# A recommender tower on one core: low parts of three tables on GpSimd, a second lookup in pieces, six groups of rows turned between the products

## The chip, the cores and the metric

The kernel runs on one NeuronCore of a Trainium2 chip. The metric is the device time of one execution, in microseconds (us), lower is better. Three executions of the kernel before took 121.43, 120.68 and 122.37 us; the median is 121.43 us. The engines are TensorE (PE in the profile, its weight loads PEld), VectorE (DVE), ScalarE (ACT), GpSimd (POOL) and SyncE (SP, which issues transfers).

## The reference, cut to what matters

```python
# ids (512, 26); tbl_f (1000, 1250, 12500 or 125000 rows, 128), float32; dense (512, 128)
e = jnp.stack([tbl_f[ids[:, f]] for f in range(26)], axis=1)      # (512, 26, 128)
combined = jnp.concatenate([dense[:, None, :], e], axis=1)        # (512, 27, 128)
interactions = jnp.einsum('bnd,bmd->bnm', combined, combined)     # 27 x 27 per sample
z = jnp.concatenate([dense, interactions[:, TRIU_I, TRIU_J]], axis=1)
h = jnp.concatenate([z, dense], axis=1)                           # (512, 607)
h = jnp.maximum(h @ W_top1 + b_top1, 0.0)                         # 512 wide
h = jnp.maximum(h @ W_top2 + b_top2, 0.0)                         # 256 wide
y = h @ W_top3                                                    # (512, 1)
```

## The kernel before, in words

**Fifteen tables by products with one-hot matrices.** The 15 tables with 1000 or 1250 rows (`ONEHOT_TABLES`) are looked up on PE. Table number h is loaded whole, with 125 partitions of 8 or 10 rows each (`CHUNKS`). DVE compares the ids with row numbers (L544) and makes all chunks of the one-hot matrix but the last, which ACT makes (L620, L625). Tables that share one comparison form a unit (`UNITS`), and there are two buffers of one-hot matrices (`UNIT_RING`). To keep float32 precision each table is cut in two: ACT rounds it into a HIGH part (L610), and DVE subtracts that from the table, which gives the LOW part (`make_low`, L553, two halves per table). A lookup of a table of 8 chunks is 16 matmuls of 128 x 512: HIGH of the first half, LOW of the first half, HIGH of the second, LOW of the second (`lookup`, L355). There are two buffers of parts (`WORK_RING`) and four of tables (`TABLE_RING`): SP loads table h + 4 when both LOW halves of table h are made. ACT copies each finished lookup from PSUM into `xt` (L631). The last lookup (h = 14) is made in two pieces of 256 samples each (`COLUMNS`), so that the products of the first samples can start between parts of the second piece.

**Eleven tables by gathers.** GpSimd gathers rows of the other 11 tables with indirect transfers (L327), 4 tiles of 128 samples x 11 = 44 of them, in order. The rows are turned on PE by 3 or 4 transposes per group (`turn_group`, L370), 12 groups in all, 3 per tile; ACT copies each group into `xt` (L638). There are two PSUM banks for groups: group g may be turned once group g - 2 is copied. `AFTER_LOOKUP` lists which group is turned after which lookup, `BETWEEN_PRODUCTS` those turned later.

**Products and layers.** Each tile of 128 samples has 128 products 27 x 27 on PE in four quarters (`gram`, L392). DVE transposes the result of a tile in 32 x 32 blocks (L571) and packs the triangle (L576); the first quarter of the next tile waits for that transpose, since the PSUM banks are the same. PE turns z (`turn_z`, L403), ACT copies it (L647), and the three layers follow (L416 and L426, L440 or L453, L466), tile by tile, woven into the products of the tiles behind.

**Order.** Every engine works through a list written in the program, in order, and waits on semaphores. On GpSimd the list is the four row-number instructions and then the 44 gathers back to back; gather number n (from n = 6, every third) may not start before a certain lookup is done (`GATHERS_AHEAD`, `GATHERS_PER_LOOKUP`).

Of the kernel before, what the change touches and what calls it, by code (L numbers as in the profile page):

```python
# [57 lines left out]
UNITS = [[0], [1, 2], [3], [4, 5], [6], [7, 8], [9], [10, 11], [12], [13, 14]]  # L58
# [25 lines left out]
COLUMNS = [[(0, B)]] * (NOH - 1) + [[(0, B // 2), (B // 2, B)]]  # L84
PIECES = NOH + 1
# [11 lines left out]
AFTER_LOOKUP = [[], [], [], [0], [1], [2], [3], [4], [5], [], [6], [7], [8], [9], []]  # L97
BETWEEN_PRODUCTS = [10, 11]
# [51 lines left out]
def build(nc, dense_by_column, ids, ids_by_table, tables, w1, w2, columns, identity, out):  # L150
    with ExitStack() as ctx:
# [123 lines left out]
        def _(sp):  # L275
            def load_table(h):
# [7 lines left out]
                if h >= TABLE_RING:  # L284
                    sp.wait_ge(part_ready[LOW], 2 * (h - TABLE_RING + 1))
# [47 lines left out]
        def _(pe):  # L333
            def lookup(h, piece=0, quarters=range(4)):
# [5 lines left out]
                if h + piece >= 2 and 0 in quarters:  # L340
                    pe.wait_ge(lookup_copied, h + piece - 1)
                for half in range(2):
                    for part in PARTS:
# [4 lines left out]
                        else:  # L348
                            pe.wait_ge(part_ready[LOW], 2 * h + 1 + half)
                        for c in range(half * chunks // 2, (half + 1) * chunks // 2):  # L350
# [176 lines left out]
        def _(dve):  # L527
# [73 lines left out]
        def _(act):  # L601
# [137 lines left out]
```

## Time and profile before

| what | value |
|---|---|
| three runs, median | 121.43 us (120.68 to 122.37) |
| profiled execution, its own time | 120.86 us |
| its span, first to last instruction | 118.8 us |
| mean granted TensorE clock | 0.971 of full |
| PE busy | 110.5 us, 93% |
| DVE busy | 72.8 us, 61% |
| ACT busy | 59.2 us, 50% |
| POOL busy | 52.5 us, 44% |

The profile is of one execution; times in it are counted from the start of its span. The shares are means over stages with different limits: lookups until 71 us, products of the first two tiles until 87 us, then the rest of the products and the layers.

### The profile page before, as it was taken

How to read it: one execution, taken by the hardware profiler on the slowest of the kernel's cores; microseconds unless marked ns; L12 is line 12 of the kernel's file. 1: busy time of each engine (PE TensorE's matmuls, PEld its weight loads, DVE VectorE, ACT ScalarE, POOL GpSimd, SP SyncE). 2: the span in 40 equal slices, each digit the busy share in tenths (PEclk: the TensorE clock that was granted, in tenths of full speed). 3: DMA queues.
4: the chain of work that ended last, by engine and by line, in shares of the span. 5: the costliest groups of instructions: out<-in, count | busy, mean ns of one | idle time of the engine just before them, and what ended most of it. 6: DMA issues, size and time to landing. Idle time of an engine off the chain costs nothing.

```text
span 118.8 us, 3660 instructions
## 1 busy us (share of the span) xinstructions
PE 110.5 (93%) x1573; PEld 90.3 (76%) x1573; DVE 72.8 (61%) x160; ACT 59.2 (50%) x111; POOL 52.5 (44%) x52
## 2 busy tenths in 40 slices
PE   5999999979999999999997999766999999999991
PEld 2377578848888888888885899654799999999970
DVE  3799999999899997999399700070072053044020
ACT  3729967994497776790999050301020211113441
POOL 2777778778877777778777700000000000000000
PEclk9999999999999999999999999985599999999999
DMA  4899999999996799649942200000000000000000
GB/s 87 283 303 282 279 256 258 246 273 247 268 263 138 199 258 257 159 92 337 397 145 50 61 22 6 6 0 6 6 6 6 6 0 6 6 6 0 0 0 1
DMA packets 6044, 15.48 MB, mean 130 GB/s; under 512 B 1655, under 2 KB 2427, under 8 KB 5902
## 3 DMA queue, kind: packets, MB, share of 16 engines
q1 hardware_dynamic: 4452, 12.20, 36.9%
q0 software_dynamic: 1408, 2.89, 9.9%
q10 hardware_dynamic: 170, 0.18, 0.7%
q8 instruction: 12, 0.20, 0.6%
q14 instruction: 2, 0.02, 0.1%
HBM read 15.26 MB, written 0.00 MB: 129 GB/s over the span
## 4 chain that ended last, share of the span: by engine, by line
PE 83%; DVE 9%; issue 3%; DMA 2%; ACT 1%; DVEq 0%
PE ps_a L355 46%; PE ps_gram L392 10%; DVE onehot L544 6%; PE ps_rows L426 5%; PE ps_h L440 5%; PE ps_a L426 5%; PE ps_rows L370 5%; DMA idrow<-ids_by_table 2%; PE ps_rows L416 2%; PE ps_z L403 2%; PE ps_a L453 2%; DVE part_sb L553 2%; PE ps_a L416 1%; DVE table_sb L571 1%; PE ps_h L466 1%
## 5 line engine op out<-in xcount | busy, mean ns | idle before, releaser
L355 PE MATMUL ps_a<-onehot,part_sb 125*128 125x512 f32 (+1 forms) x272 | 63.6, 386 | 1.9 <-issue 1.7
L327 POOL DMA_INDIRECT rows_sb<-tbl,ids_sb x44 | 51.9, 1179 | 15.3 <-issue 13.1
L355 PEld LDWEIGHTS ps_a<-onehot,part_sb 125*128 125x128 f32 x272 | 47.7, 188 | 13.7 <-issue 4.0
L544 DVE TENSOR_SCALAR onehot<-idrow,row_id 125x512 fp32r<-125x512 int16 (+1 forms) x78 | 42.2, 602 | 2.6 <-DMA idrow<-ids_by_table 1.5
L553 DVE TENSOR_TENSOR part_sb<-table_sb,part_sb 125x512 fp32r<-125x512 f32 (+1 forms) x30 | 20.6, 716 | 2.0 <-ACT part_sb L610 2.0
L571 DVE STREAM_TRANSPOSE table_sb<-ps_gram 128x864 f32<-128x864 f32 x4 | 4.3, 1083 | 26.6 <-PE ps_gram L392 26.6
L631 ACT COPY xt<-ps_a 128x512 f32<-128x512 f32 (+1 forms) x16 | 10.0, 628 | 19.0 <-PE ps_a L355 11.9
L610 ACT CAST part_sb<-table_sb 125x1024 fp32r<-125x1024 f32 (+2 forms) x16 | 16.8, 1056 | 2.7 <-DMA table_sb<-tbl 2.7
L392 PE MATMUL ps_gram<-xt 128*27 128x27 f32 x1024 | 13.1, 201 | 2.8 <-issue 2.1
L392 PEld LDWEIGHTS ps_gram<-xt 128*27 128x27 f32 x1024 | 11.1, 114 | 5.6 <-issue 4.2
L638 ACT COPY xt<-ps_rows 128x128 f32<-128x128 f32 (+2 forms) x32 | 8.2, 340 | 5.6 <-PE ps_rows L370 5.4
L620 ACT ACTIVATE distance<-idrow,row_id 125x512 f32<-125x512 int16 (+1 forms) x10 | 9.5, 948 | 0.2 <-DMA idrow<-ids_by_table 0.2
L625 ACT ACTIVATE onehot<-distance 125x512 fp32r<-125x512 f32 (+1 forms) x10 | 8.5, 848 | 0.8
L647 ACT COPY table_sb<-ps_z 128x384 f32<-128x384 f32 x4 | 1.9, 479 | 12.0 <-PE ps_z L403 12.0
L370 PE MATMUL ps_rows<-ident_sb,rows_sb 128*128 128x128 f32 x44 | 7.2, 284 | 0.0
L370 PEld LDWEIGHTS ps_rows<-ident_sb,rows_sb 128*128 128x128 f32 x44 | 5.7, 145 | 1.4
L440 PE MATMUL ps_h<-table_sb,w_sb 128*128 128x128 f32 x48 | 6.5, 279 | 0.0
L426 PE MATMUL ps_a<-table_sb,w_sb 128*128 128x128 f32 x48 | 6.1, 279 | 0.0
L426 PE MATMUL ps_rows<-table_sb,w_sb 128*128 128x128 f32 x48 | 6.1, 279 | 0.0
L440 PEld LDWEIGHTS ps_h<-table_sb,w_sb 128*128 128x128 f32 x48 | 5.8, 192 | 0.1
L474 PE MATMUL ps_z<-zeros 128*128 128x512 bf16 x13 | 4.6, 526 | 1.2 <-DVE zeros L528 1.2
L426 PEld LDWEIGHTS ps_a<-table_sb,w_sb 128*128 128x128 f32 x48 | 5.6, 192 | 0.1
(33 smaller groups left out, 44.4 us busy)
## 6 DMA issues: line engine op xcount, KB each, us to landing
table_sb<-tbl SPq DMA_DIRECT2D x11, 448.0 KB
table_sb<-tbl SPq DMA_DIRECT2D x4, 560.0 KB
idrow<-ids_by_table SPq DMA_DIRECT2D x5, 256.0 KB
w_sb<-w SPq DMA_DIRECT2D x1, 1280.0 KB
rows_sb<-tbl,ids_sb POOLq DMA_INDIRECT x44
table_sb<-tbl SPq DMA_DIRECT2D x10, 52.0 KB
idrow<-ids_by_table SPq DMA_DIRECT2D x4, 128.0 KB
w_sb<-w SPq DMA_DIRECT2D x1, 512.0 KB
```

What stands on the lines that cost most here:

```text
L327: pool.indirect_dma_start(rows_sb[:, t % ROWS_RING, GATHERED.index(f), :], None, tables[f], bass.IndirectOffsetOnAxis(ids_sb[:, t, f:f + 1 ...
L355: last = pe.matmul(ps_a[:, (h + piece) % 2, a:b], parts_sb[part][:, w, c * D:(c + 1) * D], unit_onehot(u, c)[:, member, a:b], start=(part ...
L370: last = pe.transpose(ps_rows[:, g % 2, slot * P:(slot + 1) * P], rows_sb[:, t % ROWS_RING, GATHERED.index(n - 1), :], ident)
L392: last = pe.matmul(ps_gram[j * NPAD:j * NPAD + N, half, s * N:(s + 1) * N], x, x, start=True, stop=True)
L426: last = pe.matmul(h1_block(t, m), w1_sb[:, c, m * P:(m + 1) * P], zt[:, t % 2, c, :], start=False, stop=(c == ZC - 1), skip_group_check=True)
L440: last = pe.matmul(h2_block(t, m), w2_sb[:, k, m * P:(m + 1) * P], h1[:, t % 2, k, :], start=(k == 0 and m == 0), stop=(k == M1 - 1), skip ...
L544: dve.tensor_scalar(unit_onehot(u, c), idrow[0:VP, w, 0:n, :], row_id[0:VP, first + c:first + c + 1], None, ALU.is_equal).then_inc(onehot_ ...
L553: dve.tensor_tensor(parts_sb[LOW][:, w, columns], table_sb[0:VP, s, columns], parts_sb[HIGH][:, w, columns].bitcast(F32), ALU.subtract).th ...
L610: act.copy(parts_sb[HIGH][:, w, first:end], table_sb[0:VP, s, first:end]).then_inc(part_ready[HIGH], 1)
L620: act.activation(distance[:, 0:n, :], idrow[0:VP, w, 0:n, :], ACT.Abs, bias=row_id[0:VP, negated:negated + 1]) \
L625: act.activation(unit_onehot(u, chunks - 1), distance[:, 0:n, :], ACT.Relu, bias=1.0, scale=-1.0) \
L631: act.copy(xt[:, a // RUN:b // RUN, ONEHOT_TABLES[h] + 1, :], ps_a[:, (h + piece) % 2, a:b].rearrange("p (q r) -> p q r", r=RUN)).then_inc ...
```

## The change

GpSimd makes the LOW parts of tables h = 0, 5 and 12 (`LOW_BY_GPSIMD`), two subtractions of 125 x 512 each, put into its list ahead of its 3rd, its 20th and its 41st gather. DVE no longer makes them. The tables are reordered (table 7, of 1250 rows, moves from place 12 to place 10), so the chunks per lookup and the units change with them, and h = 12 now has 8 chunks. Lookups 13 and 14 are both made in two pieces. Six groups of rows (6 to 11) are turned behind the lookups instead of two. `GATHERS_AHEAD` goes from 6 to 9. The total number of chunks stays 128.

The list of GpSimd in the kernel before, from its branch to its end (`rows_sb` holds gathered rows, `row_id` the row numbers):

```order
L308 UNCONDITIONAL_BRANCH
L313 ISA
L313 IOTA row_id 128x8
L315 IOTA row_id 128x1
L313 IOTA row_id 128x10
L315 IOTA row_id 128x1
L327 DMA rows_sb<-tbl,ids_sb 128x128 x44
L151 UNCONDITIONAL_BRANCH
```

The same list after the change, from the last row-number instruction on (`part_sb` holds the parts, `table_sb` the tables):

```order
L336 IOTA row_id 128x1
L361 DMA rows_sb<-tbl,ids_sb 128x128 x2
L344 TENSOR_TENSOR part_sb<-table_sb,part_sb 125x512 x2
L361 DMA rows_sb<-tbl,ids_sb 128x128 x17
L344 TENSOR_TENSOR part_sb<-table_sb,part_sb 125x512 x2
L361 DMA rows_sb<-tbl,ids_sb 128x128 x21
L344 TENSOR_TENSOR part_sb<-table_sb,part_sb 125x512 x2
L361 DMA rows_sb<-tbl,ids_sb 128x128 x4
L167 UNCONDITIONAL_BRANCH
```

Six subtractions stand in the one list of GpSimd now: the pair of table 5 behind 19 gathers, the pair of table 12 behind 40.

The list of PE in the kernel before, from lookup 13 to the last quarter of tile 1 (L355 lookups, L370 transposes of groups, L392 products, L416 the dense part of layer 1, L403 the turning of z):

```order
L355 MATMUL ps_a<-onehot,part_sb 128x512 x16
L370 MATMUL ps_rows<-ident_sb,rows_sb 128x128 x4
L355 MATMUL ps_a<-onehot,part_sb 128x256 x24
L392 MATMUL ps_gram<-xt 27x27 x32
L355 MATMUL ps_a<-onehot,part_sb 128x256 x4
L392 MATMUL ps_gram<-xt 27x27 x32
L355 MATMUL ps_a<-onehot,part_sb 128x256 x4
L370 MATMUL ps_rows<-ident_sb,rows_sb 128x128 x4
L392 MATMUL ps_gram<-xt 27x27 x32
L416 MATMUL ps_a<-dense_sb,w1d 128x128 x2
L392 MATMUL ps_gram<-xt 27x27 x32
L416 MATMUL ps_a<-dense_sb,w1d 128x128 x2
```

The same place after the change, from the lookups 9 to 12 (72 matmuls, no group between them) to the second quarter of tile 1 (L389 lookups, L404 transposes, L426 products, L450 the dense part):

```order
L389 MATMUL ps_a<-onehot,part_sb 128x512 x72
L389 MATMUL ps_a<-onehot,part_sb 128x256 x44
L426 MATMUL ps_gram<-xt 27x27 x32
L389 MATMUL ps_a<-onehot,part_sb 128x256 x4
L404 MATMUL ps_rows<-ident_sb,rows_sb 128x128 x4
L426 MATMUL ps_gram<-xt 27x27 x32
L389 MATMUL ps_a<-onehot,part_sb 128x256 x8
L426 MATMUL ps_gram<-xt 27x27 x32
L404 MATMUL ps_rows<-ident_sb,rows_sb 128x128 x4
L389 MATMUL ps_a<-onehot,part_sb 128x256 x4
L426 MATMUL ps_gram<-xt 27x27 x32
L389 MATMUL ps_a<-onehot,part_sb 128x256 x4
```

The last four matmuls of the last piece now stand behind the whole of tile 0, and group 8 and then the first quarter of tile 1 follow them. On ACT the copies of groups 6 to 11 stand behind the copy of that last piece. The diff, cut to its core:

```diff
-ONEHOT_TABLES = [4, 10, 11, 0, 17, 19, 1, 20, 24, 5, 25, 3, 7, 8, 14]
+ONEHOT_TABLES = [4, 10, 11, 0, 17, 19, 1, 20, 24, 5, 7, 25, 3, 8, 14]
-CHUNKS = [8] * 3 + ([10] + [8] * 2) * 4
+CHUNKS = [8] * 3 + ([10] + [8] * 2) * 2 + [10] * 2 + [8] * 4
-UNITS = [[0], [1, 2], [3], [4, 5], [6], [7, 8], [9], [10, 11], [12], [13, 14]]
+UNITS = [[0], [1, 2], [3], [4, 5], [6], [7, 8], [9], [10], [11, 12], [13, 14]]
+LOW_BY_GPSIMD = {0: 2, 5: 19, 12: 40}
...
-COLUMNS = [[(0, B)]] * (NOH - 1) + [[(0, B // 2), (B // 2, B)]]
+SPLIT = 2
+COLUMNS = [[(0, B)]] * (NOH - SPLIT) + [[(0, B // 2), (B // 2, B)]] * SPLIT
...
-AFTER_LOOKUP = [[], [], [], [0], [1], [2], [3], [4], [5], [], [6], [7], [8], [9], []]
-BETWEEN_PRODUCTS = [10, 11]
+AFTER_LOOKUP = [[], [], [0], [1], [2], [], [3], [4], [5], [], [], [], [], [], []]
+BETWEEN_PRODUCTS = [6, 7, 8, 9, 10, 11]
-GATHERS_AHEAD = 6
+GATHERS_AHEAD = 9
...
@@ SP, load_table
-                    sp.wait_ge(part_ready[LOW], 2 * (h - TABLE_RING + 1))
+                    sp.wait_ge(low_ready(h - TABLE_RING), low_number(h - TABLE_RING, 1))
@@ GpSimd
+            def make_low(h):
+                s, w, middle = h % TABLE_RING, h % WORK_RING, CHUNKS[h] // 2 * D
+                if h >= WORK_RING:
+                    pool.wait_ge(lookup_done, h - WORK_RING + 1)
+                for half, columns in enumerate((slice(0, middle), slice(middle, CHUNKS[h] * D))):
+                    pool.wait_ge(part_ready[HIGH], rounded(h, half))
+                    pool.tensor_tensor(parts_sb[LOW][:, w, columns], table_sb[0:VP, s, columns],
+                                       parts_sb[HIGH][:, w, columns].bitcast(F32), ALU.subtract) \
+                        .then_inc(low_by_gpsimd_ready, 1)
...
+                    for h, gather in LOW_BY_GPSIMD.items():
+                        if gather == issued:
+                            make_low(h)
@@ PE, lookup
-                            pe.wait_ge(part_ready[LOW], 2 * h + 1 + half)
+                            pe.wait_ge(low_ready(h), low_number(h, half))
@@ PE, behind the lookups
-            lookup(NOH - 1, 1, [0, 1])
+            lookup(before, 1, [0, 1, 2])
             gram(0, 0)
-            lookup(NOH - 1, 1, [2])
+            lookup(before, 1, [3])
+            turn_group(BETWEEN_PRODUCTS[0])
             gram(0, 1)
-            lookup(NOH - 1, 1, [3])
-            turn_group(BETWEEN_PRODUCTS[0])
+            lookup(last, 1, [0, 1])
             gram(0, 2)
-            layer1_dense(0, 0)
+            turn_group(BETWEEN_PRODUCTS[1])
+            lookup(last, 1, [2])
             gram(0, 3)
-            layer1_dense(0, 1)
+            lookup(last, 1, [3])
+            turn_group(BETWEEN_PRODUCTS[2])
             gram(1, 0)
-            turn_group(BETWEEN_PRODUCTS[1])
+            for k in range(2):
+                layer1_dense(0, k)
             gram(1, 1)
-            layer1_dense(1, 0)
+            turn_group(BETWEEN_PRODUCTS[3])
             gram(1, 2)
             turn_z(0)
+            for g in BETWEEN_PRODUCTS[4:]:
+                turn_group(g)
             gram(1, 3)
-            layer1_dense(1, 1)
+            for k in range(2):
+                layer1_dense(1, k)
@@ DVE
-            dve.wait_ge(part_ready[LOW], 2 * NOH)
+            dve.wait_ge(part_ready[LOW], 2 * (NOH - len(LOW_BY_GPSIMD)))
+            dve.wait_ge(low_by_gpsimd_ready, 2 * len(LOW_BY_GPSIMD))
```

## Rows read from the trace of the kernel before

**Rows 1.** The chain that ended last, 13 to 76 us: start, length, what.

```profile
13.02 10.04 PE ps_a L355 x42
...
24.40 0.81 issue
25.21 3.07 PE ps_a L355 x12
28.28 0.44 PE ps_rows L370 x4
28.72 3.64 PE ps_a L355 x16
32.36 0.33 PE ps_rows L370 x3
32.69 4.57 PE ps_a L355 x20
...
64.38 0.70 issue
...
68.54 2.87 PE ps_a L355 x24
71.41 0.68 PE ps_gram L392 x54
72.09 0.67 PE ps_a L355 x4
```

**Rows 2.** The same chain, 76 us to the layers.

```profile
76.56 1.04 issue
...
77.85 1.09 DVE table_sb L571
...
81.53 1.09 issue
82.62 0.34 PE ps_gram L392 x9
82.95 1.16 PE ps_rows L416 x4
84.11 0.90 PE ps_gram L392 x64
85.01 0.83 PE ps_z L403 x3
...
87.30 1.34 PE ps_a L426 x12
...
94.67 0.89 PE ps_a L416 x8
...
100.67 0.48 PE ps_z L403 x3
```

**Rows 3.** Stretches: us, PE, PEld, DVE, ACT, POOL busy (instructions), granted clock, DMA share, GB/s.

```profile
74.00:77.00 3.00, 2.56 (x137) 2.13 (x134) 0.00 (x0) 1.13 (x4) 0.00 (x0) 1.00 0.02 5
77.00:79.00 2.00, 0.85 (x5) 0.63 (x5) 1.11 (x2) 0.00 (x0) 0.00 (x0) 1.00 0.00 0
79.00:81.00 2.00, 1.92 (x95) 1.56 (x99) 1.00 (x9) 0.23 (x1) 0.00 (x0) 0.64 0.03 8
81.00:83.00 2.00, 0.91 (x57) 0.73 (x45) 0.00 (x0) 0.31 (x1) 0.00 (x0) 0.50 0.00 0
83.00:85.00 2.00, 2.00 (x69) 1.72 (x69) 0.00 (x0) 0.00 (x0) 0.00 (x0) 0.50 0.03 8
85.00:87.00 2.00, 2.00 (x72) 1.63 (x71) 0.26 (x1) 0.48 (x1) 0.00 (x0) 0.65 0.00 0
```

**Rows 4.** Waits: engine and line, whom it waited for, us, times, longest.

```profile
POOL rows_sb L327 <- issue: 13.1, 43, 0.3
```

**Rows 5.** Timeline of POOL: gathers 1, 11, 19, 20, 40 and 41 of 44.

```profile
3.46 1.12 POOL L327 DMA_INDIRECT rows_sb<-tbl,ids_sb  x1 [2.22 <-DMA ids_sb<-ids]
...
18.48 2.26 POOL L327 DMA_INDIRECT rows_sb<-tbl,ids_sb  x1 [0.30 <-issue]
...
31.32 1.56 POOL L327 DMA_INDIRECT rows_sb<-tbl,ids_sb  x1 [0.30 <-issue]
33.19 1.02 POOL L327 DMA_INDIRECT rows_sb<-tbl,ids_sb  x1 [0.30 <-issue]
...
62.23 1.02 POOL L327 DMA_INDIRECT rows_sb<-tbl,ids_sb  x1 [0.30 <-issue]
63.55 1.02 POOL L327 DMA_INDIRECT rows_sb<-tbl,ids_sb  x1 [0.30 <-issue]
```

**Rows 6.** Groups by form: line, engine, operation, count; busy us, mean ns; idle before.

```profile
L327 POOL DMA_INDIRECT rows_sb<-tbl,ids_sb x44 | 51.9, 1179 | 15.3 <-issue 13.1 <-DMA ids_sb<-ids 2.2
...
L553 DVE TENSOR_TENSOR part_sb<-table_sb,part_sb 125x512 fp32r<-125x512 f32 x22 | 14.4, 680 | 0.0
```

**Rows 7.** Timeline of DVE: comparisons for two tables of 8, a pair of subtractions.

```profile
19.84 4.72 DVE L544 TENSOR_SCALAR onehot<-idrow,row_id 125x1024 fp32r<-125x1024 int16 x7
24.48 1.28 DVE L553 TENSOR_TENSOR part_sb<-table_sb,part_sb 125x512 fp32r<-125x512 f32 x2
```

**Rows 8.** Timeline of ACT: copies of a piece and of a group of four.

```profile
68.87 0.79 ACT L638 COPY xt<-ps_rows 128x128 f32<-128x128 f32 x4
70.50 0.40 ACT L631 COPY xt<-ps_a 128x256 f32<-128x256 f32 x1 [0.83 <-PE ps_a L355]
```

**Rows 9.** Stretch 8.8 to 13.7 us, columns as in rows 3.

```profile
8.80:13.70 4.90, 4.73 (x19) 2.86 (x18) 4.90 (x9) 4.84 (x6) 3.99 (x4) 1.00 1.04 264
```

More of the change, by code:

```diff
@@ L74 @@
         _places[_c] = _places.get(_c, []) + [(_members[0], half)]
+    _places = {_c: [(h, half) for h, half in halves if h not in LOW_BY_GPSIMD] for _c, halves in _places.items()}
     LOW_BEFORE.append(_places)
     _owed = _members[1:]
-LOW_AT_END = [(h, half) for h in _owed for half in range(2)]
+LOW_AT_END = [(h, half) for h in _owed for half in range(2) if h not in LOW_BY_GPSIMD]
 VP_A = VP // 16 * 16
@@ L82, with place @@
 ROWS_RING = 2
-COLUMNS = [[(0, B)]] * (NOH - 1) + [[(0, B // 2), (B // 2, B)]]
-PIECES = NOH + 1
+SPLIT = 2
+COLUMNS = [[(0, B)]] * (NOH - SPLIT) + [[(0, B // 2), (B // 2, B)]] * SPLIT
+PIECES = NOH + SPLIT
+def place(h, piece):
+    return h + SPLIT * piece
 GATHERED = [f for f in range(F) if f not in ONEHOT_TABLES]
@@ L103, with low_number @@
 GATHERS_PER_LOOKUP = 3
-GATHERS_AHEAD = 6
+GATHERS_AHEAD = 9
 HIGH, LOW = PARTS = range(2)
+def low_number(h, half):
+    same = [x for x in range(h) if (x in LOW_BY_GPSIMD) == (h in LOW_BY_GPSIMD)]
+    return 2 * len(same) + 1 + half
 def rounded(h, half):
@@ L217, in build @@
         part_ready = [sem(f"part{i}_ready") for i in PARTS]
+        low_by_gpsimd_ready = sem("low_by_gpsimd_ready")
         lookup_done = sem("lookup_done")
@@ L234, in build, with low_ready @@
         stored = sem("stored")
+        def low_ready(h):
+            return low_by_gpsimd_ready if h in LOW_BY_GPSIMD else part_ready[LOW]
         def unit_onehot(u, c):
@@ L339, in lookup @@
                 a, b = COLUMNS[h][piece]
-                if h + piece >= 2 and 0 in quarters:
-                    pe.wait_ge(lookup_copied, h + piece - 1)
+                if place(h, piece) >= 2 and 0 in quarters:
+                    pe.wait_ge(lookup_copied, place(h, piece) - 1)
                 for half in range(2):
@@ L354, in lookup @@
                                 pe.wait_ge(last_onehot_ready, u + 1)
-                            last = pe.matmul(ps_a[:, (h + piece) % 2, a:b], parts_sb[part][:, w, c * D:(c + 1) * D],
+                            last = pe.matmul(ps_a[:, place(h, piece) % 2, a:b], parts_sb[part][:, w, c * D:(c + 1) * D],
                                              unit_onehot(u, c)[:, member, a:b], start=(part == HIGH and c == 0),
@@ L381, in gram @@
                     pe.wait_ge(group_copied, GROUPS_UP_TO[t])
-                    pe.wait_ge(lookup_copied, NOH + (t >= TILES // 2))
+                    pe.wait_ge(lookup_copied, NOH if t < TILES // 2 else PIECES)
                     if t == 0:
@@ L480, in _ @@
                     turn_group(g)
-            lookup(NOH - 1, 1, [0, 1])
+            before, last = NOH - 2, NOH - 1
+            lookup(before, 1, [0, 1, 2])
             gram(0, 0)
-            lookup(NOH - 1, 1, [2])
+            lookup(before, 1, [3])
+            turn_group(BETWEEN_PRODUCTS[0])
             gram(0, 1)
-            lookup(NOH - 1, 1, [3])
-            turn_group(BETWEEN_PRODUCTS[0])
+            lookup(last, 1, [0, 1])
             gram(0, 2)
-            layer1_dense(0, 0)
+            turn_group(BETWEEN_PRODUCTS[1])
+            lookup(last, 1, [2])
             gram(0, 3)
-            layer1_dense(0, 1)
+            lookup(last, 1, [3])
+            turn_group(BETWEEN_PRODUCTS[2])
             gram(1, 0)
-            turn_group(BETWEEN_PRODUCTS[1])
+            for k in range(2):
+                layer1_dense(0, k)
             gram(1, 1)
-            layer1_dense(1, 0)
+            turn_group(BETWEEN_PRODUCTS[3])
             gram(1, 2)
             turn_z(0)
+            for g in BETWEEN_PRODUCTS[4:]:
+                turn_group(g)
             gram(1, 3)
-            layer1_dense(1, 1)
+            for k in range(2):
+                layer1_dense(1, k)
             for t in range(TILES - 2):
@@ L628, in copy_lookup @@
             def copy_lookup(h, piece=0):
-                act.wait_ge(lookup_done, h + piece + 1)
+                act.wait_ge(lookup_done, place(h, piece) + 1)
                 a, b = COLUMNS[h][piece]
                 act.copy(xt[:, a // RUN:b // RUN, ONEHOT_TABLES[h] + 1, :],
-                         ps_a[:, (h + piece) % 2, a:b].rearrange("p (q r) -> p q r", r=RUN)).then_inc(lookup_copied, 1)
+                         ps_a[:, place(h, piece) % 2, a:b].rearrange("p (q r) -> p q r", r=RUN)).then_inc(lookup_copied, 1)
             def copy_group(g):
@@ L693, in _ @@
                     copy_group(g)
-            copy_lookup(NOH - 1, 1)
+            for h in range(NOH - SPLIT, NOH):
+                copy_lookup(h, 1)
             for g in BETWEEN_PRODUCTS:
```

## The prediction

> **What bounds the kernel now.** I read the chain that ended last first [rows 1]. From 13.02 us on it is PE: lookups at 3.64 us per 16 matmuls, which is 0.2275 us each, transposes of groups at 0.44 for four. Two gaps "issue" stand in it, 0.81 at 24.40 and 0.70 at 64.38; in both PE stands between the HIGH and the LOW matmuls of a lookup, so I read them as waits for a LOW part. So until 71 us PE is the limit and DVE comes close to it.
>
> Behind that stage PE loses more [rows 2]: 1.04 at 76.56, a wait for DVE's transpose (1.09 at 77.85), 1.09 at 81.53. The granted clock falls too [rows 3]: 0.64, 0.50, 0.50 and 0.65 in the four stretches from 79 to 87 us. PE had been busy 0.85 of 2.00 us ahead of it. At that level (1.2 GHz) a quarter of products took 0.90 us instead of 0.68, three transposes of z 0.83 instead of 0.48, the dense four 1.16 where eight took 0.89 later. Over the whole low stretch I put the loss at 2.5 us. With 2.8 us of gaps (1.04, 1.09 and 0.6 of the wait for DVE) the change has 5.3 us to win there.
>
> Last I read GpSimd's own line, because the change puts work into its list. It waits for nothing: 43 idle times of 0.30 us each [rows 4], so its 44 gathers run back to back from 3.46 us, mean 1179 ns [rows 5, 6]. The 20th starts at 33.19 and the 41st at 63.55: a 44% share of the span, yet a full list until 68 us.
>
> **GpSimd's chain, the term that decides.** The subtractions of table 5 stand where gather 20 stood, those of table 12 where gather 41 stood. No row has a subtraction on GpSimd. The bounds: DVE's same operation on the same shape takes 680 ns [rows 6]; the longest thing GpSimd does, a gather, 2.26 us [rows 5]. I take 1.2 us each with its gap, the mean of what that engine did here: a software-driven engine is nearer to its own row than to DVE's. The Trainium skill (GPSIMD Engine Reference, § Performance versus the Vector engine) gives 4497 ns for 2048 float32 elements of a tensor_tensor; a quarter is an estimate of 1.12 us, and by it the forecast falls by five times 0.08.
>
> - LOW of table 5, first half: 33.19 + 2 x 1.2 (table 0's pair, ahead of it) + 1.2 = 36.8 us.
> - LOW of table 12, first half: 63.55 + 4 x 1.2 + 1.2 = 69.55 us.
>
> When does PE want them? Lookup 5 ran from 28.72; its LOW matmuls come after four HIGH ones, at 29.63. Group 2 (0.33) is now ahead of it, and up to 0.8 is saved before, at the gap of 24.40 or the start. So PE wants table 5 at 28.8 to 30.0 and stands still about **7 us**. All that DVE's relief gives before this point (the subtractions of tables 0 and 5, 1.28 us a pair [rows 7]) is lost in that wait.
>
> From 36.8 at the full clock: the other 12 matmuls 2.73; lookups 6, 9 and 10 of 20 matmuls at 4.57; 7, 8 and 11 at 3.64; three groups 0.44 + 0.44 + 0.33; four HIGH of lookup 12, 0.91. Sum 29.5, so PE is at table 12's LOW at 66.3, and 69.55 is 3.3 us later. The clock will surely have fallen in a wait of 7 us, when 2.3 us of gaps were enough before. The low stretch before is 6.8 us long by rows 3; lookups at half the clock would lose at most 3.4 us in it. That loss fits into the 3.3 us of the second wait, so I cost it at nothing: GpSimd hides it. Queued behind: DVE's one-hot matrices run ahead by two units in the waits and then keep pace (a unit of two tables of 8 costs it 4.72 + 2 x 1.28 = 7.3 us [rows 7], as much as PE). SP's load of table 9 waits for table 5's LOW and comes some 6 us late, but its rounding is wanted at 50 us. The w1 load behind table 14 comes later too and is wanted only near 77.
>
> **After 69.55.** The other 12 matmuls of lookup 12: 2.73, so 72.3. Then 44 matmuls of 256 columns; 24 of them took 2.87, so 0.12 each, 5.27: the first products start at 77.55 instead of 71.41, **6.1 us later**. Splitting lookup 13 costs only 16 x (0.24 - 0.2275) = 0.2, and 0.2 per switch to products, inside these terms.
>
> From there to layer 1 (87.30 before, so 15.9 us): eight quarters of products at 0.68 = 5.4; pieces of 4, 8, 4 and 4 matmuls 3.2; 22 transposes at 0.11 = 2.4; the dense part 2 x 0.89 = 1.8; turning z 0.5. That is 13.3. One wait is new: group 8 may be turned only when group 6 is copied, and ACT copies it behind the last piece: 0.40 + 0.79 us [rows 8], 1.2 in all. DVE's transpose of tile 0 (1.09) runs under it. The gaps "issue" at 76.56 and 81.53 I let go, since products now lie between other work. With the clock up this stage takes 14.5 us, 1.4 less than before. Behind it both kernels do the same.
>
> Sum against the profiled execution's own 120.86 us: + 6.1 - 1.4 = 125.6. The median of the runs is 0.6 above that execution, so for the runs I say **126.0 us**, 3.8% slower. (Two per cent, 119.0 to 123.9, is about what a measurement of this kernel can tell from no change.)
>
> **Rivals.**
>
> 1. *GpSimd's subtractions are blocked by DVE.* At 2.26 us each, five of them lie 5.3 us later: 131. Against: between 8.8 and 13.7 us DVE was busy 4.90 of 4.90 us [rows 9] and four gathers took 3.99 us there. For: those gathers don't read two tables out of SBUF. During the pair of table 5 DVE should be idle itself. The Trainium skill (SBUF — State Buffer, § Who interferes with whom) says that a VectorE instruction in a 2-port mode, or with two SBUF inputs against a GpSimd instruction that reads SBUF, blocks the other for its whole length; by that rule each subtraction among comparisons could begin one DVE instruction late. Chance 0.15.
>
> 2. *The clock falls a second time.* If it is up again soon after 37 us, PE reaches table 12 at 67, waits 2 to 3 us and starts the pieces and products at the low level; by a loss of 2.5 (as before) to 3.4 us this gives 128.5 to 129.5. Chance 0.12.
>
> 3. *The gathers get shorter, and it is not slower.* A gather of 1.02 us with its gap is 1.32; the first 19 took 29.7 us, which is 4.6 more than 19 x 1.32, the first 40 took 60.1, which is 7.3 more. What makes some of them long I can't tell; the DMA share is at 1.04 in the first stage [rows 9], so it may be the transfers. If PE's wait thins these out, the chain shortens with them. Without any long gather, table 5 comes at 32.1, table 12 at 62.3, and the sum is 7.3 less: 118.7 for the runs, which is 2% faster. It decides from the point where that excess falls by half: then 122.3, within 2%. Against: the load of SP in the first 30 us is the same as before. Chance 0.08 for all of it, 0.10 for about half.
>
> 4. *The relief works as written:* GpSimd has the LOW parts before PE asks. Then only the gains are left, some 118. It would need 19 gathers and three subtractions by 29 us; at 1.32 and DVE's own 0.68 they end at 30.6. Not given a chance of its own.
>
> **How the numbers follow.** The forecast of 126 has 0.55. Its own range: GpSimd at 0.68 us would put table 12 at 66.9, but the slowed PE is there only at 68 to 69, so it can't fall below some 124.4; with long gathers a few tenths longer it reaches 127.5. The range for 8 in 10 takes in half of rival 3 below and most of rival 1 above: 122.0 to 131.0. Slower by over 2%: forecast and rivals 1 and 2, less a little, 0.79. Within 2%: 0.13. Faster: 0.08.
>
> **What would show it.** In the timeline of POOL, a pair of TENSOR_TENSOR behind gather 2, gather 19 (near 35.5 to 38 us) and gather 40 (near 68.3 to 70.8); their mean tells rival 1. In the chain of waits, a step to POOL's line L344 twice, and PE's line L389 waiting for it, near 7 us and up to 3.3 us. In the stretches, a granted clock of 0.5 after 33 us, full again by 44 us, and full from 79 to 93 us. PE should wait about 1.2 us at group 8 for ACT. If PE doesn't wait for table 5, or the gathers 3 to 19 end before 32 us, the forecast is wrong; if it waits as said and the time still isn't up by 3%, then the stage between the lookups and the layers gave back more than I count.

## The result, and the profile after

The changed kernel took 129.4 us (median of four runs, 128.6 to 129.93) against 121.36 us (120.68 to 122.37) for the kernel before: a ratio of 1.065, 95% interval 1.056 to 1.074. It is 6.5% slower; the forecast was 126.0 us with a range of 122.0 to 131.0. Medians here and below are of all runs of a kernel; ratios leave out runs more than 1.5% above its fastest. The profiled execution took 129.36 us, with a span of 127.6 us (118.8 before) and a mean granted clock of 0.973 (0.971 before).

First the page: busy time of each engine, and the granted clock in 40 slices of 3.19 us.

```profile
PE 113.9 (89%) x1589; PEld 92.0 (72%) x1589; DVE 73.0 (57%) x154; ACT 59.2 (46%) x112; POOL 60.0 (47%) x58
...
PEclk9999999999756999999999999999999999999999
```

DVE has six instructions less and is busy no shorter (72.8 before). The clock falls in slices 11 to 13, not near 80 us as before. The groups of section 5 and the views by form show the new operation, and what DVE did with its relief:

```profile
L344 POOL TENSOR_TENSOR part_sb<-table_sb,part_sb 125x512 fp32r<-125x512 f32 x6 | 7.6, 1285 | 0.3 <-ACT part_sb L652 0.2
...
L585 DVE TENSOR_SCALAR onehot<-idrow,row_id 125x1024 fp32r<-125x1024 int16 x35 | 27.5, 852 | 9.6 <-PE ps_a L389 8.3 <-DMA idrow<-ids_by_table 1.4
...
L594 DVE TENSOR_TENSOR part_sb<-table_sb,part_sb 125x512 fp32r<-125x512 f32 x16 | 10.5, 679 | 0.4 <-ACT part_sb L652 0.4
```

A subtraction takes 1285 ns on GpSimd. Six fewer on DVE are 3.9 us less than the 14.4 of [rows 6]. But the comparisons take 27.5 us for 35; the same 35 take 24.1 in a kernel that does without GpSimd's subtractions (first experiment). 3.4 of the 3.9 us are given back.

GpSimd's list, beside [rows 5]: the two pairs that PE waits for.

```profile
33.90 2.50 POOL L344 TENSOR_TENSOR part_sb<-table_sb,part_sb 125x512 fp32r<-125x512 f32 x2
...
67.65 2.52 POOL L344 TENSOR_TENSOR part_sb<-table_sb,part_sb 125x512 fp32r<-125x512 f32 x2
```

They run behind gathers 19 and 40, as written. The chain that ended last, to the start of the layers, beside [rows 1, 2]:

```profile
33.90 1.28 POOL part_sb L344
35.19 0.04 issue
35.23 10.04 PE ps_a L389 x32
...
64.75 7.31 DVE onehot L585 x7
72.06 0.60 DVE part_sb L594
72.67 0.04 issue
72.71 5.05 PE ps_a L389 x40
77.76 0.68 PE ps_gram L426 x52
...
84.57 0.45 issue
...
85.44 0.38 ACT xt L673
85.82 0.68 ACT xt L680 x4
86.50 0.04 issue
86.55 0.55 PE ps_rows L404 x3
...
87.77 1.09 PE ps_a L450 x8
...
89.42 0.73 issue
...
93.37 0.27 issue
...
95.15 1.34 PE ps_a L460 x12
```

Products start at 77.76 instead of 71.41, layer 1 at 95.15 instead of 87.30, and the span ends at 127.6 instead of 118.8. So the 8.8 us are 6.35 before the products, 1.5 in their first stage and 0.95 behind it. The chain's last leg ahead of the products is DVE's: its comparisons at 64.75 ran beside GpSimd's second pair, and its LOW part for lookup 13 came 0.24 us after PE could have used it. PE's own timeline at the two places, with the wait in brackets:

```profile
35.23 5.06 PE L389 MATMUL ps_a<-onehot,part_sb 125*128 125x512 f32 x11 [4.61 <-POOL part_sb L344]
...
68.99 3.48 PE L389 MATMUL ps_a<-onehot,part_sb 125*128 125x512 f32 x16 [0.84 <-POOL part_sb L344]
72.71 5.05 PE L389 MATMUL ps_a<-onehot,part_sb 125*128 125x256 f32 x40 [0.24 <-DVE part_sb L594]
```

Columns of the stretches are those of [rows 3]:

```profile
33.00:36.00 3.00, 0.77 (x2) 0.67 (x3) 0.00 (x0) 0.00 (x0) 2.98 (x3) 0.62 0.17 44
36.00:39.00 3.00, 3.00 (x9) 2.32 (x8) 0.00 (x0) 0.00 (x0) 2.31 (x3) 0.50 0.50 151
```

PE works through 36 to 39 us at the low level (0.50, 1.2 GHz); it had stood idle for 4.61 us before. The 32 matmuls that take 7.3 us at 0.2275 each took 10.04.

### The profile page after: what moved, and what is told of

Read it like the earlier page. It is cut to its first block, busy times and chain, and to the rows that moved or that the text cites. A ratio compares the mean times of both kernels' runs of the same rounds, so it can differ in the third digit from the quotient of the medians.

```text
span 127.6 us, 3698 instructions
## 1 busy us (share of the span) xinstructions
PE 113.9 (89%) x1589; PEld 92.0 (72%) x1589; DVE 73.0 (57%) x154; ACT 59.2 (46%) x112; POOL 60.0 (47%) x58
## 4 chain that ended last, share of the span: by engine, by line
PE 61%; DVE 19%; POOL 6%; DMA 5%; issue 5%; ACT 1%; DVEq 0%
PE ps_a L389 28%; DVE onehot L585 16%; PE ps_gram L426 9%; DMA idrow<-ids_by_table 5%; POOL rows_sb L361 5%; PE ps_rows L460 5%; PE ps_h L474 5%; PE ps_a L460 5%; PE ps_rows L404 3%; DVE part_sb L594 3%; PE ps_a L487 2%; PE ps_a L450 2%; PE ps_rows L450 2%; PE ps_z L437 1%; POOL part_sb L344 1%
## 5 line engine op out<-in xcount | busy, mean ns | idle before, releaser
L389 PE MATMUL ps_a<-onehot,part_sb 125*128 125x512 f32 (+1 forms) x288 | 67.1, 385 | 7.3 <-POOL part_sb L344 5.4
L389 PEld LDWEIGHTS ps_a<-onehot,part_sb 125*128 125x128 f32 x288 | 50.8, 195 | 20.6 <-POOL part_sb L344 6.7
L585 DVE TENSOR_SCALAR onehot<-idrow,row_id 125x512 fp32r<-125x512 int16 (+1 forms) x78 | 45.6, 648 | 11.3 <-PE ps_a L389 8.7
L594 DVE TENSOR_TENSOR part_sb<-table_sb,part_sb 125x512 fp32r<-125x512 f32 (+1 forms) x24 | 16.7, 724 | 1.1 <-ACT part_sb L652 1.1
L426 PE MATMUL ps_gram<-xt 128*27 128x27 f32 x1024 | 12.9, 194 | 1.5 <-issue 1.5
L426 PEld LDWEIGHTS ps_gram<-xt 128*27 128x27 f32 x1024 | 10.7, 107 | 4.2 <-issue 2.5
L404 PE MATMUL ps_rows<-ident_sb,rows_sb 128*128 128x128 f32 x44 | 6.8, 277 | 1.2 <-ACT xt L680 1.1
L344 POOL TENSOR_TENSOR part_sb<-table_sb,part_sb 125x512 fp32r<-125x512 f32 x6 | 7.6, 1285 | 0.3 <-ACT part_sb L652 0.2
L404 PEld LDWEIGHTS ps_rows<-ident_sb,rows_sb 128*128 128x128 f32 x44 | 5.1, 141 | 2.5 <-ACT xt L680 1.3
L508 PE MATMUL ps_z<-zeros 128*128 128x512 bf16 x13 | 5.5, 617 | 1.2 <-DVE zeros L569 1.2
```

The costliest lines, as they stand in the source:

```text
L344: pool.tensor_tensor(parts_sb[LOW][:, w, columns], table_sb[0:VP, s, columns], parts_sb[HIGH][:, w, columns].bitcast(F32), ALU.subtract) \
L389: last = pe.matmul(ps_a[:, place(h, piece) % 2, a:b], parts_sb[part][:, w, c * D:(c + 1) * D], unit_onehot(u, c)[:, member, a:b], start=(p ...
L404: last = pe.transpose(ps_rows[:, g % 2, slot * P:(slot + 1) * P], rows_sb[:, t % ROWS_RING, GATHERED.index(n - 1), :], ident)
L426: last = pe.matmul(ps_gram[j * NPAD:j * NPAD + N, half, s * N:(s + 1) * N], x, x, start=True, stop=True)
L585: dve.tensor_scalar(unit_onehot(u, c), idrow[0:VP, w, 0:n, :], row_id[0:VP, first + c:first + c + 1], None, ALU.is_equal).then_inc(onehot_ ...
L594: dve.tensor_tensor(parts_sb[LOW][:, w, columns], table_sb[0:VP, s, columns], parts_sb[HIGH][:, w, columns].bitcast(F32), ALU.subtract).th ...
```

## The experiments

All ratios are against the kernel before, run on the same chip beside each kernel, with 95% intervals. Its medians there lay between 121.72 and 122.52 us.

### Is it the part of GpSimd, or the new order?

**Everything of the change but GpSimd's subtractions.** DVE makes all LOW parts.

```diff
-LOW_BY_GPSIMD = {0: 2, 5: 19, 12: 40}
+LOW_BY_GPSIMD = {}
-            dve.wait_ge(low_by_gpsimd_ready, 2 * len(LOW_BY_GPSIMD))
```

> The change with all LOW parts made by VectorE again (no subtraction on GpSimd); the order of tables, the second lookup in pieces and the six groups between the products stay. Theory (GpSimd's list is what made the change slow): TensorE's wait of 4.6 us at table 5 and of 0.8 at table 12 are gone, the clock doesn't fall at 33 us, the comparisons that took 7.4 us beside GpSimd's subtractions take 4.7 again, and the first products start near 71 us instead of 77.7: 122 to 124 us. Rival (the new order behind the lookups is itself the loss): 126 us or more.

Measured: 120.43 us, ratio 0.984 (0.976 to 0.992), below the 122 to 124 that I had expected: the new order alone gains 1.6%. Products start at 68.28, 3.1 us before [rows 1]. Some 1.7 of that are the 15 transposes of groups that no longer stand between lookups, and the two waits for DVE are 0.31 and 0.24 instead of 0.81 and 0.70. Behind the lookups it loses again; PE's timeline there, at group 8:

```profile
77.37 0.60 PE L404 MATMUL ps_rows<-ident_sb,rows_sb 128*128 128x128 f32 x3 [1.15 <-ACT xt L679]
...
78.80 2.08 PE L450 MATMUL ps_a<-dense_sb,w1d 128*128 128x128 f32 x8
```

The wait for ACT comes 0.4 us behind a gap of 0.71 (75.13 to 75.84), and then the clock is at 0.50 from 78 to 81 us: the dense eight take 2.08 instead of 1.09. So without GpSimd's part the order pays, even with this loss in it.

**The reverse: the kernel before, with GpSimd's subtractions alone**, at the same three places and with `GATHERS_AHEAD` at 9 (`make_low` and its waits are those of the change; table 12 has 10 chunks here).

```diff
+LOW_BY_GPSIMD = {0: 2, 5: 19, 12: 40}
-GATHERS_AHEAD = 6
+GATHERS_AHEAD = 9
```

> The kernel before with the change's first part alone: LOW parts of tables 0, 5 and 12 by GpSimd at the same places in its list (and 9 gathers ahead); tables, pieces and groups as before. Table 12 has 10 chunks here, so its subtractions are of 125 x 640. Theory (that part alone is the whole loss): TensorE waits 4 to 5 us at table 5, reaches table 12 near GpSimd's 69 us, first products near 80 us, 128.5 to 131.5 us. Rival (the new order shares in the loss): under 127 us.

Measured: 132.26 us, ratio 1.091 (1.080 to 1.103), a little above the range that I had given. PE waits 4.75 us at table 5 and only 0.31 at table 12, but DVE comes late behind it:

```profile
66.72 7.80 DVE L578 TENSOR_SCALAR onehot<-idrow,row_id 125x1024 fp32r<-125x1024 int16 x7 [1.94 <-PE ps_a L389]
```

These seven took 4.72 in [rows 7]. They run beside GpSimd's pair (66.86, 3.11 us long), and PE then waits 1.70 us for DVE's LOW part at 75.16. So GpSimd's part alone costs 9.1%, more than the whole change: the order gives some back. (Part of that is table 12's pair, which is of 125 x 640 here.)

### Are the waits a matter of the place in GpSimd's list?

**Table 5's pair five gathers earlier**, then **table 12's pair four gathers earlier**, then **both**:

```diff
-LOW_BY_GPSIMD = {0: 2, 5: 19, 12: 40}
+LOW_BY_GPSIMD = {0: 2, 5: 14, 12: 40}
```

> The pair of table 5 stands behind 14 gathers instead of 19, that of table 12 still behind 40. Theory (one chain on GpSimd, and table 12's place in it is the wall): the wait at table 5 is gone (TensorE wants it near 30 us, GpSimd has it near 28.5), but TensorE then waits for table 12 until 69 us all the same, some 6 to 7 us long, and the clock falls in that wait, so that pieces and products run at 1.2 GHz: 129 to 132 us, no gain. Rival (each wait adds its own length): 129.4 less 4.6 and the 2.8 us lost by the clock, 122 us.

Measured: 131.67 us, ratio 1.077 (1.068 to 1.085). No wait at table 5, and the whole of it at table 12:

```profile
70.04 5.22 PE L389 MATMUL ps_a<-onehot,part_sb 125*128 125x512 f32 x14 [8.48 <-POOL part_sb L344]
```

Removing the larger wait of the two brought no gain. PE reached the second place earlier, stood there longer, and paid for the clock behind it (0.50 until 72 us, 0.62 from 72 to 75).

```diff
-LOW_BY_GPSIMD = {0: 2, 5: 19, 12: 40}
+LOW_BY_GPSIMD = {0: 2, 5: 19, 12: 36}
```

> The pair of table 12 stands behind 36 gathers instead of 40, that of table 5 still behind 19. Theory: the wait at table 5 stays (4.6 us), and so does the fall of the clock behind it; TensorE comes to table 12 near 68 us and finds it made: 0.8 us less, and up to 1 us more where the comparisons of the last unit are no longer held up at the same place: 127.5 to 129 us. Rival (table 12's subtraction holds VectorE, which is the real wall): 126 us or less.

Measured: 127.86 us (126.43 to 129.12, too scattered for an interval) beside 122.17. Table 5 still stops PE for 3.60 us, table 12 no longer, and products start at 75.47, 2.2 us before those of the change; the next wait, behind it, is for DVE:

```profile
70.48 5.06 PE L389 MATMUL ps_a<-onehot,part_sb 125*128 125x256 f32 x40 [0.81 <-DVE part_sb L594]
```

```diff
-LOW_BY_GPSIMD = {0: 2, 5: 19, 12: 40}
+LOW_BY_GPSIMD = {0: 2, 5: 14, 12: 36}
```

> Table 5 behind 14 gathers and table 12 behind 36. Theory: neither wait is left, the clock stays up in the lookups, the first products start near 71 to 72 us: 122 to 124.5 us. Rival (GpSimd's subtractions hold VectorE for their whole length, 1.28 us each, six of them): the lookups stay late by some 3 to 5 us, 125.5 to 128 us.

Measured: 127.03 us, ratio 1.038 (1.031 to 1.046). I had expected neither wait. But PE now comes to table 12 some 6 us earlier, and for that place 36 is still too late:

```profile
65.74 9.98 PE L389 MATMUL ps_a<-onehot,part_sb 125*128 125x512 f32 x56 [3.49 <-POOL part_sb L344]
```

My expectation had judged the new place by the old time of the reader.

**Place 32 for table 12**, so that nobody waits for GpSimd:

```diff
-LOW_BY_GPSIMD = {0: 2, 5: 19, 12: 40}
+LOW_BY_GPSIMD = {0: 2, 5: 14, 12: 32}
```

> Table 5 behind 14 gathers, table 12 behind 32. GpSimd should then have table 12 before TensorE wants it near 62 us. Theory (both waits were the loss, and VectorE pays for each subtraction of GpSimd with its length while it has little of that to spare): no wait for GpSimd above 0.5 us, first products at 69 to 71.5 us, 121 to 124 us, no better than with all LOW parts on VectorE (120.4). Rival (the relief of VectorE is worth something once it comes in time): 119 us or less.

Measured: 121.97 us (ten runs), ratio 1.005 (1.001 to 1.009). The waits for GpSimd are gone, and with them almost all of the loss. Still it is slower than the same order with no subtraction on GpSimd (0.984). The profile of DVE shows why:

```profile
26.45 6.32 DVE L585 TENSOR_SCALAR onehot<-idrow,row_id 125x512 fp32r<-125x512 int16 x9
...
57.65 6.87 DVE L585 TENSOR_SCALAR onehot<-idrow,row_id 125x1024 fp32r<-125x1024 int16 x7
```

Nine such comparisons take 3.70 where GpSimd only gathers, seven of the wide form 4.72. They ran beside GpSimd's two pairs and took 2.6 and 2.15 us longer; each pair had relieved DVE of 1.28. Over the whole kernel DVE's comparisons take 48.6 us, where they take 42.2 with no subtraction on GpSimd, and its subtractions of 125 x 512 take 10.4 instead of 14.5: 6.4 us more for 4.1 less. So well-timed pairs cost DVE more than they save it, and PE waits 0.84 us for DVE ahead of 65.17.

**Keep PE busy in the first wait.** The changed kernel, with 16 products of zeros ahead of PE's wait for table 5:

```diff
+                        elif h == 5 and half == 0:
+                            for _ in range(16):
+                                pe.matmul(ps_z[:, 0, :], zeros[:, 0:P], zeros[:, :], start=True, stop=True)
+                            pe.wait_ge(low_ready(h), low_number(h, half))
```

> The change as it is, with 16 more matmuls of 512 columns on zeros put ahead of TensorE's wait for table 5's LOW part (3.5 us of the 4.6 us wait), their result unused. Theory (table 12's place in GpSimd's list is the wall, so what the clock costs ahead of it is hidden): the clock stays up at 33 to 41 us, the 32 matmuls behind the wait take 7.3 instead of 10.0 us, TensorE waits some 3.5 us at table 12 instead of 0.8, first products still near 77.5 us, and the clock may fall there instead: 128.5 to 131.5 us. Rival (the slow clock behind the first wait is part of the loss): 126 to 127.5 us.

Measured: 132.29 us, ratio 1.083 (1.074 to 1.091), above the 128.5 to 131.5 expected and far from the rival's 126 to 127.5.

```profile
35.24 7.59 PE L393 MATMUL ps_a<-onehot,part_sb 125*128 125x512 f32 x32 [1.10 <-POOL part_sb L344]
...
69.14 11.03 PE L393 MATMUL ps_a<-onehot,part_sb 125*128 125x512 f32 x56 [3.50 <-POOL part_sb L344]
```

The clock stayed up (1.00 from 33 to 36 us) and the 32 matmuls took 7.59 instead of 10.04. But PE resumed at table 12 at 69.14, as without them (68.99): the 2.5 us were spent waiting there. So the step of the prediction that costs the first clock loss at nothing is shown to be right. The new wait of 3.50 us then brought the clock down (0.50 from 69 to 72 us) just before the products, which start at 80.10: that is the second fall of rival 2, and its price comes on top. In the change itself this fall did not happen (1.00 from 69 to 72 and from 77 to 96 us).

### Who blocks whom?

**Six subtractions on GpSimd that nobody waits for**, added to the order with DVE making all (the first experiment), at places 2, 19 and 40, on memory of their own.

```diff
+                    for _ in range(2 if issued in (2, 19, 40) else 0):
+                        pool.wait_ge(idle_done, idle)
+                        pool.tensor_tensor(idle_out[0:VP, :], idle_in[0:VP, :], idle_in[0:VP, :],
+                                           ALU.subtract).then_inc(idle_done, 1)
+                        idle += 1
```

> VectorE makes all LOW parts, and GpSimd makes six subtractions of 125 x 512 on a buffer of its own that nobody waits for, at the change's places (ahead of gathers 3, 20 and 41). So only the place in the list and the sharing with VectorE are left of the suspected cost. Theory (a subtraction on GpSimd holds VectorE for its length): single comparisons or subtractions of VectorE beside them grow by 1.3 to 2.6 us, GpSimd's own stay at 1.28, gathers end some 8 us later; in time 0.5 to 3 us more than without them (120.4). Rival (VectorE is not held): its operations keep their lengths, and the time stays at 120 to 121.

Measured: 124.77 us, ratio 1.029 (1.021 to 1.037), where the same kernel without them has 0.984. Work on GpSimd that nobody uses costs 4.5 points, more than I had expected; the products start at 72.83 instead of 68.28. It is not that gathers come later: PE waits for none of them, but 4.0 us in all for DVE's LOW parts. DVE's timeline and then GpSimd's:

```profile
3.47 5.09 DVE L592 TENSOR_SCALAR onehot<-idrow,row_id 125x512 fp32r<-125x512 int16 x7 [1.38 <-DMA idrow<-ids_by_table]
...
34.45 5.94 DVE L592 TENSOR_SCALAR onehot<-idrow,row_id 125x1024 fp32r<-125x1024 int16 x7 [0.28 <-PE ps_a L396]
...
67.22 3.44 DVE L601 TENSOR_TENSOR part_sb<-table_sb,part_sb 125x512 fp32r<-125x512 f32 x2 [0.49 <-ACT part_sb L658]
```

```profile
6.04 2.24 POOL L364 TENSOR_TENSOR idle_out<-idle_in 125x512 f32<-125x512 f32 x2
33.15 3.37 POOL L364 TENSOR_TENSOR idle_out<-idle_in 125x512 f32<-125x512 f32 x2
67.61 2.50 POOL L364 TENSOR_TENSOR idle_out<-idle_in 125x512 f32<-125x512 f32 x2
```

Without them the three rows of DVE read 2.90, 4.73 and 1.28: +2.2, +1.2 and +2.2 us. At 67.61 DVE's second subtraction waits while GpSimd's pair keeps its 2.50; at 33.15 both pay, GpSimd 0.9 and DVE 1.2. The Trainium skill (SBUF — State Buffer, § Who interferes with whom) has the port pair as an exclusive lock held for a whole instruction by whoever issued first, and a tensor_tensor with both inputs in SBUF as one that contends with GpSimd's reads. The third pair agrees: 3.44 against 1.28. For the comparisons, with one input in SBUF, the page allows it only in a 2-port mode; no row names the mode they run in. The rows do show that they work at twice the rate of the subtractions: a comparison takes 0.26 us more for 512 more columns (0.67 against 0.41), a subtraction 0.13 us more for 128 (0.81 against 0.68).

### The stage behind the lookups

**Groups 7 and 8 each turned one place later** in the order with DVE making all, so that ACT's copies are done when PE wants the bank:

```diff
             gram(0, 2)
-            turn_group(BETWEEN_PRODUCTS[1])
             lookup(last, 1, [2])
             gram(0, 3)
             lookup(last, 1, [3])
-            turn_group(BETWEEN_PRODUCTS[2])
+            turn_group(BETWEEN_PRODUCTS[1])
             gram(1, 0)
+            turn_group(BETWEEN_PRODUCTS[2])
             for k in range(2):
                 layer1_dense(0, k)
```

> As the version in which VectorE makes all LOW parts, with groups 7 and 8 turned one place later: 7 behind the last piece, 8 behind the first quarter of tile 1. Theory (TensorE's 1.15 us at group 8 is ScalarE's copying of group 6 behind the last piece): that wait is gone, 0.2 to 0.5 us of waiting for VectorE's transpose of tile 0 comes in its place, and with less idling the clock may stay up between 79 and 86 us, worth up to 2.5 us: 117.5 to 120 us. Rival (TensorE only waits elsewhere for ScalarE, since all copies stand behind that piece): 120 to 121 us, as before the edit.

Measured: 118.15 us (117.75 to 119.87), ratio 0.973 (0.963 to 0.983): the fastest kernel of the study. PE no longer waits for ACT's copies and the clock is 1.00 for the whole span of 115.7 us. What is left are gaps with no releaser inside runs of products:

```profile
78.79 0.31 PE L426 MATMUL ps_gram<-xt 128*27 128x27 f32 x14 [0.80 <-issue]
...
82.55 0.42 PE L426 MATMUL ps_gram<-xt 128*27 128x27 f32 x29 [0.53 <-issue]
```

The first comes behind 50 of 64 matmuls of that quarter, the second behind 35, and the changed kernel has its gaps of 0.73 and 0.27 at the same two counts.

**Shift PE's list by 64 instructions** in that kernel (three warm-up matmuls fewer, 35 tiny ones more, each with its weight load), to see whether the gaps belong to data or to the place in the code:

```diff
-            for _ in range(WARM_UP):
+            for _ in range(WARM_UP - 3):
...
+            for _ in range(35):
+                pe.matmul(ps_z[:, 0, 0:NPAD], zeros[:, 0:P], zeros[:, 0:NPAD], start=True, stop=True)
```

> The fastest version so far (VectorE makes all LOW parts, group 8 behind the first quarter of tile 1; 118.15 us) with 3 of the 13 warm-up matmuls taken away and 35 of 32 columns put in their place, so that 64 more TensorE instructions (32 matmuls and their weight loads) lie ahead of everything. In that version, in the one with group 8 earlier and in the change, gaps that nothing releases stand at the same points of TensorE's list: 50 matmuls into the second quarter of tile 1, 35 into its fourth. Theory (they come with the loading of TensorE's code in blocks of 16 KB): the gaps move 32 matmuls earlier in the list, to about 18 and 3 matmuls into those quarters; time 117.5 to 119.5 us. Rival (they belong to the place: a PSUM bank or a copy): they stay at 50 and 35.

Measured: 119.89 us, ratio 0.979 (0.974 to 0.984).

```profile
80.09 0.59 PE L426 MATMUL ps_gram<-xt 128*27 128x27 f32 x46 [1.09 <-issue]
...
83.85 0.72 PE L426 MATMUL ps_gram<-xt 128*27 128x27 f32 x61 [0.50 <-issue]
```

The gaps moved by 32 matmuls, behind 18 and behind 3. The time is a little above what I had expected, and above that of the kernel without the shift, because more gaps come to light: they add up to 3.8 us here (1.10 at 71.51 in tile 0, 0.36 at 87.88 and 0.71 at 100.12 besides these two), 1.9 us there. The run with PE kept busy in the first wait has 16 more matmuls ahead of everything, and shifts the two gaps by 16, from behind 50 and 35 to behind 34 and 19:

```profile
92.05 0.42 PE L430 MATMUL ps_gram<-xt 128*27 128x27 f32 x30 [1.12 <-issue]
...
96.08 0.59 PE L430 MATMUL ps_gram<-xt 128*27 128x27 f32 x45 [0.81 <-issue]
```

So the gaps belong to the place in PE's list, not to an operand. Neighbouring gaps stand 126 to 128 matmuls apart, which is 252 to 256 instructions with their weight loads. A page of the profile lists a queue "instruction" with 12 transfers of some 16 KB (0.20 MB), in the kernels before and after alike, and 13 in the shifted one. This is what the DMA engines of the changed kernel move from 85 to 100 us, in 40 slices of 0.375 us; all of it is of that queue:

```profile
GB/s 0 0 0 0 0 0 0 44 0 0 0 0 0 0 0 0 44 0 0 0 0 0 0 0 0 0 0 44 0 0 0 0 0 0 0 0 0 0 44 0
```

The transfers are at 87.7, 91.35, 95.3 and 99.6 us, and PE comes out of its gaps at 90.15, 93.64 and 101.83: 2.2 to 2.5 us behind a transfer each time (the third transfer is followed by no gap). In the fastest kernel the delay is 2.5 to 2.6 us for all three gaps, in the kernel before 2.2 and 2.3. And from the end of one gap to the end of the next, where nothing else stops PE, pass 3.5 to 4.0 us: 90.15 to 93.64 in the change, 75.05 to 78.79 and 78.79 to 82.55 in the fastest kernel, 80.09 to 83.85 and 92.05 to 96.08 in the rows above. The work between them is 2.9 to 3.3 us. So what PE waits for is its code: place, spacing and time agree, though no run changed the loading itself. The Trainium skill (Runtime: NRT & Kernel Launch, § Instruction fetch mechanics) says that code is refilled in blocks of 16 KiB, 256 instructions, and that the cost of crossing one is "mostly hidden". The spacing agrees with that; among products of 27 columns the gaps of 0.50 to 1.10 us are not hidden.

**One lookup in two pieces instead of two**, the dense part of tile 0 moved ahead of tile 1 to fill the place:

```diff
-SPLIT = 2
+SPLIT = 1
...
```

> As the fastest version (VectorE makes all LOW parts, six groups between the products, group 8 late), but only lookup 14 in pieces, as before the change, and the dense part of tile 0 put between its last quarter and tile 1, where it covers VectorE's transpose. 32 TensorE instructions fewer. If the second lookup in pieces is what covers the copies and the transpose, this one loses 0.5 to 1.5 us: 118.7 to 119.7 us. If the six groups alone do it, it stays at 117 to 118.5 us, and the second split was not needed.

Measured: 119.16 us (118.75 to 119.6), ratio 0.979 (0.972 to 0.986). Products start at 68.97, 1.2 us later, and one gap is long:

```profile
79.95 0.33 PE L404 MATMUL ps_rows<-ident_sb,rows_sb 128*128 128x128 f32 x1 [2.10 <-issue]
```

The intervals overlap, so the worth of the second split isn't settled. The gaps add up to 3.1 us here (0.21, 2.10, 0.83) and to 1.9 in the fastest kernel, a difference as large as that of the two times. The long gap fits the same step: its end is 3.84 us behind that of the gap before it (76.11 to 79.95), and only 1.7 us of that were work.

## Why the prediction was right, point by point

The direction and the two waits were right, and so was the start of the products to 0.2 us. The size was less good: 129.4 lies above the 124.4 to 127.5 that I gave the forecast's own case. It is inside the wide range only because that range makes room for rivals 1 and 2, and it equals the price of rival 2 (128.5 to 129.5) by luck, since no second fall of the clock took place. Of the 3.8 us between 125.6 and 129.36 for the profiled execution, 2.9 are in the stage of the first products, 0.95 behind it and 0.2 ahead of it; the time outside the span is 0.3 us shorter than before.

- **GpSimd's subtraction.** Forecast 1.2 us, measured 1.285 as the mean of one and 1.25 in the last two pairs. The Trainium skill (GPSIMD Engine Reference, § Performance versus the Vector engine) gave an estimate of 1.12; the trace has 0.16 more.
- **Table 5.** Its LOW half forecast for 36.8, measured 35.18; gathers 3 to 19 took 24.9 us (8.96 to 33.90), where the same 17 took 26.4 before (6.47 to 32.88). That is a small part of rival 3; I had it as a case of its own and not as a term. PE asked at 30.62 (forecast 28.8 to 30.0), so the wait was 4.61 us and not 7.
- **The relief at the start** was no gain. I had let it bring PE up to 0.8 us forward, but PE's lookups behind the start go on at 14.00 instead of 13.02 (13.48 in the new order with all LOW parts on DVE). With table 0's LOW parts off its list DVE waits for its ids (1.36 us, until 7.67), and the four comparisons then run beside GpSimd's first pair and take 3.68 instead of 2.74.
- **The clock.** It fell in the first wait as said and cost 2.7 us (10.04 for 7.3), hidden by the wait for table 12. The run with PE kept busy shows it: 2.5 us faster there, and no earlier at table 12.
- **Table 12.** Forecast 69.55, PE resumed at 68.99. The products: forecast 77.55, measured 77.76. Two small misses cancel there: PE went on 0.6 us earlier, and needed 8.8 us to the products instead of 8.0, 0.24 of it the wait for DVE.
- **The stage to layer 1** was the term mis-sized: "14.5 us, 1.4 less than before", measured 17.4, so 1.5 more. By the chain: gaps that I let go 1.45 (0.45, 0.73, 0.27); quarters of products 5.98 instead of 5.4; 22 transposes 2.93 instead of 2.4; the dense part 2.18 instead of 1.8. The wait at group 8, forecast 1.2, was 1.15, and the clock stayed up. Five of the eight quarters took the 0.68 that I had counted; of the other three (0.89, 0.87 and 0.82) two hold a gap, and in the first a block of code ends by the count of 126 to 128 matmuls. So 2.0 of the 2.9 us are breaks at places in the code, which work laid between products does not close. The other 0.9 come from taking each duration from wherever it stood: the dense eight take 1.09 us behind products and 0.89 behind layer 2 (at 103.22 in the same chain), four transposes 0.59 behind products at 90.46 and 0.44 behind a lookup at 79.11.
- **Behind it** I forecast no change; it took 32.45 us (95.15 to 127.6) instead of 31.5. A new gap of 0.49 at 101.34 is half of this.
- **Rival 1** was right in that the two engines block each other and wrong in its victim. In the change GpSimd kept its 1.25 us, but the comparisons took longer, four at 7.67 as said above and seven here, where 4.72 is their time beside gathers:

```profile
64.68 7.39 DVE L585 TENSOR_SCALAR onehot<-idrow,row_id 125x1024 fp32r<-125x1024 int16 x7
```

That cost little here only because PE was late already: DVE's LOW part came 0.24 us after PE wanted it. Remove the wall (places 36 and 32), and DVE is the next wait: 0.81 and 0.84 us.
- **Rival 4**, the relief as written, I had at some 118. With the places right it gives 121.97: being ready in time is not enough, because the relief itself is void.

Open stays why some gathers take 1.5 to 2.7 us where most take 1.02, what makes up the 2.2 to 2.9 us between a transfer of code and PE's next instruction, and the worth of the second split.

## What to carry to other kernels

A step put into the list of an engine that is never idle is a deadline for its reader: work out when the reader comes in the new kernel, not in the old one. Two waits in one chain hide each other, and also what the first does to the clock, so removing the larger alone may gain nothing. Don't take a total inside the range for a proof of the sum: here the term called decisive was off by 0.2 us and the one called small by 2.9. Before moving elementwise work from DVE to GpSimd, look for DVE instructions beside it: here a pair of 2.5 us on GpSimd took up to 2.7 us of DVE's time to save it 1.28. And when work moves behind a stage, read the list of the engine that empties its buffer.

## What the runs showed of the hardware

- DVE's work hardly slows GpSimd's gathers: with table 5's pair early, four from 58.71 us on take 1.02 us each beside a busy DVE, and the four from 64.01 on take 0.94 each while it stands idle. But GpSimd's subtractions and DVE hold each other up for whole instructions: 3.44 us of DVE for 1.28, and 3.37 of GpSimd for 2.50.
- Gaps of 0.2 to 2.1 us stand at fixed places in PE's list in stages of small products, 126 to 128 matmuls apart where two follow each other. They moved by 32 and by 16 matmuls when the list ahead of them grew by 32 and 16. They came to 1.9 us in the fastest kernel (0.57, 0.80, 0.53).
- Each of these gaps ended 2.2 to 2.9 us behind a transfer of 16 KB of the queue "instruction", and the ends of neighbouring gaps are 3.5 to 4.0 us apart: a block of 127 matmuls that has less work than that (2.9 to 3.3 us, and 1.7 ahead of the longest gap) leaves PE idle for the rest.
